# Gated cross-attention and a mixture of experts on one core: one transfer for means and factors, an earlier second batch, a rearranged passage

## The reference, cut to what matters

```python
# per batch: keys and values come from both the context and the rows
xn = layernorm(ctx, gamma_media, beta_media)          # (256, 256)
ln = layernorm(layernorm(x), gamma_lat, beta_lat)     # (256, 256)
q = ln @ Wq + bq;  k, v = split(concat([xn, ln]) @ Wkv + bkv)   # 8 heads of 128
attn = softmax(q @ k.T * 128 ** -0.5)                 # (256, 512) per head
x = x + tanh(g_xattn) * (attn @ v @ Wo + bo)
# mixture of experts, top 2 of 8, F = 1024
xh = layernorm(x)
w, idx = softmax(top_k(xh @ Wg + bg, 2))
y = sum over the two experts e of w_e * (silu(xh @ W1[e] + b1[e]) @ W2[e] + b2[e])
x = x + tanh(g_ffn) * y
```

## Time and profile before

| | |
|---|---|
| median of 3 runs | 1546.45 us (1545.08 to 1552.04) |
| the profiled execution | 1541.18 us, its span 1539.5 us |
| busy | PE 1491.3 us (97%), DVE 1140.1 (74%), ACT 954.1 (62%), POOL 568.9 (37%) |
| mean granted clock of TensorE | 0.994 |
| a 1 MB load of expert weights, issue to landing | 18.7 us (median of 45) |

### The profile page before, as it was taken

The page is one execution under the profiler, slowest core; times in us unless marked ns, Lnnn a source line. Parts: engine busy times, 40 slices in busy tenths (PEclk is TensorE's granted clock), DMA queues, the critical chain, the costliest instruction groups (busy, mean ns, idle before and its releaser), DMA issues. The chain is left out here.

```text
span 1539.5 us, 29848 instructions
## 1 busy us (share of the span) xinstructions
PE 1491.3 (97%) x10326; PEld 1371.1 (89%) x10326; DVE 1140.1 (74%) x2749; ACT 954.1 (62%) x2057; POOL 568.9 (37%) x654
## 2 busy tenths in 40 slices
PE   8699999999999999999999999999889999999996
PEld 6588898888888888888888989888889999999996
DVE  7567877778777787777778778787686666666685
ACT  6455556556555655655555565655787777777775
POOL 4213334233243333334233342332455454444442
PEclk9999999999999999999999999999999999999999
DMA  5101101011010111101011010012854455545463
GB/s 163 46 14 49 42 22 36 22 49 42 22 35 22 37 36 33 42 21 36 22 49 42 22 36 22 8 57 63 222 122 132 128 146 142 128 128 152 133 175 81
DMA packets 84465, 106.92 MB, mean 69 GB/s; under 512 B 25658, under 2 KB 69495, under 8 KB 84191
## 3 DMA queue, kind: packets, MB, share of 16 engines
q1 hardware_dynamic: 68350, 85.98, 18.1%
q0 software_dynamic: 15824, 18.98, 6.9%
q10 hardware_dynamic: 144, 0.05, 0.0%
HBM read 86.64 MB, written 18.35 MB: 68 GB/s over the span
## 5 line engine op out<-in xcount | busy, mean ns | idle before, releaser
L921 POOL TENSOR_SCALAR probs<-probs,rsum 128x512 f32<-128x512 f32 x256 | 175.1, 695 | 609.9 <-DVE rsum L1598 603.1
L1131 ACT ACTIVATE pt_hi<-turn 128x512 fp32r<-128x512 f32 x256 | 139.5, 597 | 235.1 <-PE turn L1278 233.6
L946 POOL DMA_INDIRECT out_rows<-yo,token x71 | 119.7, 1686 | 206.0 <-DMA out_rows<-yo,token 136.4
L1715 DVE TENSOR_TENSOR ht_lo<-hs,ht_hi 128x512 fp32r<-128x512 f32 x142 | 98.2, 692 | 119.6 <-ACT ht_hi L1098 117.9
L1030 ACT ACTIVATE probs<-score,nbias 128x512 f32<-128x512 f32 x256 | 173.6, 688 | 7.1 <-DVE nbias L1594 7.1
L1592 DVE TENSOR_REDUCE smax<-score 128x1 f32<-128x512 f32 x256 | 168.1, 683 | 7.0 <-PE score L188 6.8
L1089 ACT ACTIVATE hs<-ph,vecs 128x256 f32<-128x256 f32 (+1 forms) x284 | 114.8, 460 | 93.9 <-PE ph L188 86.2
L1835 DVE TENSOR_TENSOR pt_lo<-turn,pt_hi 128x512 fp32r<-128x512 f32 x256 | 164.3, 683 | 9.4 <-ACT pt_hi L1131 8.8
L186 PE MATMUL py<-w_hi,ht_lo 128*128 (+1 forms) x568 | 162.7, 286 | 4.2 <-DVE ht_lo L1715 2.6
L188 PE MATMUL py<-w_hi,ht_hi 128*128 (+1 forms) x568 | 160.6, 283 | 0.0
L187 PE MATMUL py<-w_lo,ht_hi 128*128 (+1 forms) x568 | 160.5, 283 | 0.0
(11 more groups left out here) (243 smaller groups left out, 4685.4 us busy)
## 6 DMA issues: line engine op xcount, KB each, us to landing
w_raw<-in_L_ffn_W SPq DMA_DIRECT2D x45, 1024.0 KB, 18.7
spread<-mean_and_factor SPq DMA_DIRECT2D x15, 512.0 KB, 4.1
xhat_rows<-rows SPq DMA_DIRECT2D x16, 264.0 KB, 2.2
x_raw<-in_x SPq DMA_DIRECT2D x16, 256.0 KB, 3.0
c_raw<-in_ctx SPq DMA_DIRECT2D x16, 256.0 KB, 3.3
out_rows<-x SPq DMA_DIRECT2D x16, 256.0 KB
z_turned<-in_x_turned SPq DMA_DIRECT2D x15, 256.0 KB, 3.8
z_turned<-in_ctx_turned SPq DMA_DIRECT2D x15, 256.0 KB, 4.2
```

What stands on the lines that cost most here:

```text
L921: last = pool.tensor_scalar(probs[n % 2][:, t, :], probs[n % 2][:, t, :], rsum[:, n % 2, t:t + 1], 1.0, ALU.mult, ALU.mult)
L946: pool.indirect_dma_start(out=A["out"], out_offset=bass.IndirectOffsetOnAxis(ap=token[:, u:u + 1].bitcast(U32), axis=0), in_=yo_of(t)[:, s ...
L1131: act.activation(pt[0][:, 2 * t:2 * t + 2, :], turn[t][:, :].rearrange("p (j i) -> p j i", j=2), ACT.Copy).then_inc(s_pthi, 1)
L1715: dve.tensor_tensor(lo[:, :], hs[n % N_HS][:, :], hi[:, :].bitcast(F32), ALU.subtract).then_inc(s_hlo, 1)
```

## The change

1. **One transfer.** `spread` becomes (128 partitions, 2, 4) a batch: `norms` goes out as it lies, in one DMA, and is read back broadcast. VectorE reads it with a stride of 8 elements. The halves of `zin` change places to match.
2. **Second batch sooner.** `load(2)` goes ahead of `spread_norms(1)`. For batch 1: centre and normalise in steps 2 and 3, scale in step 3, `split_kv(1)` in step 4.
3. **Queries' weights in three pieces.** `q1` covers 2 heads, a new `q2` 4 heads. High parts: o0 and q2 in step 1, o1 in step 2. Low parts: o0 in step 1, q2 in step 2, o1 in step 4.
4. **Passage.** In step 127 TensorE turns tile 0 ahead of the probabilities, ScalarE does `hi_x(0)` and two W2 pieces ahead of its output unit, VectorE `lo_x(0)` and `take_weights(0)` ahead of its own; `find_places(14)` and `take_weights(1)` move to step 128. `norm_rows(15)` splits: VectorE makes variance plus epsilon, GpSimd only the power, VectorE the two normalised rows. GpSimd issues `gather(2)` ahead of `list_tokens(14)`, `gather(3)` and `gather(4)` ahead of `list_tokens(15)`. Counts are read at n = 6 instead of 7, `find_rows` becomes `count_rows` (n = 7) and `find_late_rows` (n = 8), `weigh` goes to n = 9. Tile 5's split stands ahead of the W1 pieces in its step.
5. **W2 over time.** Pieces of places 2 to 7 are split over n = 15 to 63, the loads of places 4 to 7 are issued later, `out` waits only for the places that a tile can need.
6. **Additions.** A tile's two scatters have a semaphore each and wait for the tile before, not for one another.

```diff
+W2_SPLIT = {1: (1, 5), 2: (15, 19), 3: (20, 26), 4: (26, 32), 5: (32, 40), 6: (40, 48), 7: (48, 64)}
+W2_LOAD = {2: 5, 4: 6, 6: 7}
+W2_NEED = {1: 3, 3: 5, 5: 6, 7: 7, 11: 8}
...
-                for tiles, cols in ((slice(0, TT), slice(T, KEYS)), (slice(TT, JT), slice(0, T))):
-                        for r in range(2):
-                            sp.dma_start(dram["spread"][c, r, cols].rearrange("(j p) -> p j", p=P), norms[:, r, tiles])\
-                                .then_inc(s_norms_out, 16)
-                sp.wait_ge(s_norms_out, 64 * c)
+                sp.dma_start(dram["spread"][c], norms[:, :, :]).then_inc(s_norms_out, 16)
+                sp.wait_ge(s_norms_out, 16 * c)
...
             load_turned(1)
+            load(2)
             spread_norms(1)
...
-                    for at in range(2, E):
-                        load_w2(at)
+                    load_w2(2)
+                    load_w2(3)
...
+                if b == B - 1:
+                    load_w2(4)
...
+            sp.wait_ge(s_gathered(EARLY), 16 * gathered(EARLY))
             load_w1(EARLY + 1)
...
+                if t - EARLY in W2_LOAD:
+                    sp.wait_ge(s_w1lo, w1_before(t - N_RAW + 1) + PARTS // 2)
+                    load_w2(W2_LOAD[t - EARLY])
...
-                if u:
-                    pool.wait_ge(s_add, 16 * u)
+                if t:
+                    for half in range(SUB):
+                        pool.wait_ge(s_add[half], 16 * added(t, half))
...
-            for s in range(SUB):
-                gather(2, s)
-            norm_rows(B - 1)
+            pool.wait_ge(s_ve_last, 1)
+            pool.tensor_tensor(rs_c[:, 0:TT], ve["c"][:, 0:TT], minus_half[:, 0:TT], ALU.pow).then_inc(s_rsc, 1)
...
+                if i == STEPS - 1:
+                    hi_x(0)
+                    for q in W2_STEPS[i]:
+                        w2_hi(q)
...
             residual(B - 1)
+            dve.wait_ge(s_mvc, B)
+            dve.tensor_scalar(ve["c"][:, 0:TT], mv_c[:, 0:TT, 1], 1.0, EPS, ALU.mult, ALU.add).then_inc(s_ve_last, 1)
             lo_h(1)
+            dve.wait_ge(s_rsc, B)
+            dve.wait_ge(s_rowst[(B - 1) % 2], 16 * ((B - 1) // 2))
+            for t in range(TT):
+                last = dve.tensor_scalar(rows[(B - 1) % 2][:, t, 0:D], x2[(B - 1) % 2][:, t, :], mv_c[:, t, 0:1],
+                                         rs_c[:, t:t + 1], ALU.subtract, ALU.mult)
+            last.then_inc(s_xn, 1)
...
-                own.mark(dve.tensor_tensor(zin[:, k, :], zin[:, k, :], spread[:, 0, :], ALU.add))
+                by_rows = zin[:, k, :].rearrange("p (j i) -> p j i", j=JT)
+                own.mark(dve.tensor_tensor(by_rows, by_rows, spread[:, :, 0, :].rearrange("p i j -> p j i"), ALU.add))
```

More of the change, by code:

```diff
@@ L543, in layer @@
         W2_BEFORE = PARTS
+        w2_need = {step_of(EARLY + t): places * PARTS for t, places in W2_NEED.items()}
         def w2_by(n):
-            return W2_BEFORE + min(W2_PIECES - W2_BEFORE, n + max(0, n - 12))
+            return W2_BEFORE + sum(min(PARTS, max(0, n + 1 - first) * PARTS // (end - first))
+                                   for first, end in W2_SPLIT.values())
         def w2_piece(at, j):
@@ L627, in turned_of, with added @@
             return (routing, ph[(FIRST_N + 2) % N_PH])[(n - FIRST_N) % 2]
+        def added(t, half):
+            return min(t, WIDE) if half else t
         def by_step(function, t):
@@ L1002, in _ @@
                     ).then_inc(s_names, 16)
-                scatter(t - 1, 0)
-                if t == 1:
-                    list_tokens(B - 1)
-            pool.wait_ge(s_add, 16 * ROWS)
+                if t == 3:
+                    for s in range(SUB):
+                        gather(EARLY + 1, s)
+                if t > 1:
+                    for s in range(subs(t - 1)):
+                        scatter(t - 1, s)
+            for half in range(SUB):
+                pool.wait_ge(s_add[half], 16 * added(N_TILES, half))
         @program("scalar")
@@ L1175, in _ @@
                     e = expert_of(act, t)
+                if n in X_SPLIT and t + 1 == EARLY:
+                    hi_x(t + 1)
                 for part in w1_parts(n + LEAD):
                     w1_hi(*part)
-                if n in X_SPLIT:
+                if n in X_SPLIT and t + 1 != EARLY:
                     hi_x(t + 1)
@@ L1656, in find_rows, with find_late_rows, do @@
                 do(dve.tensor_reduce(wide_rows[:, :], length[:, 0:E], AX_X, ALU.add))
+            def find_late_rows():
+                def do(instruction):
+                    own.mark(instruction)
+                    own.wait()
+                own.wait()
                 do(dve.tensor_scalar(wide_rows[:, :], wide_rows[:, :], -1.0, float(LATE_WIDE), ALU.mult, ALU.add))
@@ L1840, in _ @@
                     lo_h(0)
+                    find_places(B - 2)
                 for u in steps[i]:
@@ L1857, in _ @@
                     reciprocal_sum(i)
-                if i in (3, 4):
-                    normalise_turned(1, i - 3)
+                if i == STEPS - 1:
+                    lo_x(0)
+                    take_weights(0)
+                if i in (2, 3):
+                    normalise_turned(1, i - 2)
                 for u in steps[i]:
@@ L1896, in _ @@
                 t, j = TILE_OF[n]
+                if n in X_SPLIT and t + 1 == EARLY:
+                    lo_x(t + 1)
                 for part in w1_parts(n + LEAD):
@@ L1912, in _ @@
                     choose(B - 1)
+                if n == 6:
+                    read_unit("r", B - 1)
+                    find_places(B - 1)
+                if n == 7:
+                    count_rows()
                 if n == 8:
-                    find_rows()
+                    find_late_rows()
+                if n == 9:
                     weigh(B - 1)
```

119 lines of the change are left out of this document (67 added, 52 removed).

## The result

| | before | after |
|---|---|---|
| median | 1547.96 us (4 runs, 1545.08 to 1552.04) | 1522.59 us (4 runs, 1521.97 to 1524.05) |
| profiled execution, its span | 1541.18 us, 1539.5 us | 1522.59 us, 1520.9 us |

The ratio is 0.9836, 95% interval 0.981 to 0.9861: faster by 25.4 us of median, where 25.5 was forecast (1521). That agreement is better than its parts. The two profiled executions lie only 18.6 us apart; the rest is that the kernel before runs 4 to 7 us longer outside its profile and the changed one does not. In a later group of runs the same two kernels had 1544.71 (9 runs) and 1517.23 us (5 runs), 27.5 apart. In a third group one execution of the kernel before took 3424 us, and is left out of that group's ratios. What follows takes the traces apart first, and then comes back to this.

A forecast was written before the change was run, and what follows sets the result against it. TensorE was taken to bound the kernel, busy 1491.3 of 1539.5 us, so gains come from its idle time or clock. Start 15.5 plus passage 10.0 gave 25.5 off 1546.45: 1521 us, range 1515 to 1525, 1513 to 1531 with two rivals.

The forecast's parts named there:

- `kt_lo` 5.0: Steps 1 to 3 of the start: TensorE's 6.7 us of waits for `kt_lo` become 1.6, a gain of 5.0.
- The wait of 1.18: Start, step 1: TensorE's 1.18 us wait for `kt_lo` goes to about 0.1, as q1's low part shrinks.
- `kvt_lo` 7.3: Batch 1's `v` unit: the whole 7.32 us wait for `kvt_lo` goes, its rows being ready near 60 us.
- Clock 3.7: Start: without TensorE's idle stretches of 4.1 and 7.3 us, the 1.7 and 2.0 us lost to low clock return.
- floor (1.2) and ceiling (9.4): Write of `spread`: 1.2 us as an eighth of the old 9.4; 9.4 if only the count of DMAs mattered.
- the slack argument: Steady batches: VectorE idles 0.36 and 0.43 us, so the first 0.79 us of extra per step are free.
- slower by the stride: Rival, chance 0.03: strided VectorE operations cost over 0.79 us extra; from 1.25 extra the 25.5 us gain is eaten.
- Forecast 10.0: Passage, 1040 to 1160 us: 10.9 us of waits and low clock go, less 0.9 of new waits; bounds 4 and 11.
- The rival of VectorE's wait for the power: Passage, chance 0.12: slow list DMAs make `lo_x(1)` 4 to 5 us late, clock falls; gain 19.5, 1527 us.
- Zero for both: W2 pieces moved to n = 15 to 63 hide there, and GpSimd has slack for scatters: no gain or loss.
- later the only wait is 0.30 us once a batch: TensorE in attention after the start, kernel before: a single wait of 0.30 us per batch, 14 times.
- 5.3 below the median: Profiled execution of the kernel before against its runs' median; no place in the trace, so left standing in the forecast.

The follow-up runs named there:

- kernel with filler: Changed kernel plus one unused 0.68 us VectorE operation ahead of each addition and multiplication from batch 2 on, 56 in all; 1519.69 us.
- passage-only kernel: Kernel before with only the passage, W2 over time and additions changes; 1533.21 us, ratio 0.99.
- kernel with GpSimd's rows: Changed kernel with the last batch's normalised rows back on GpSimd, nothing else moved; 1522.7 us.
- with four writes: Changed kernel with means and factors again leaving in four DMAs of 4-byte pieces and VectorE reading at unit stride; 1522.62 us.
- start-only: Kernel before with only the one transfer, sooner second batch and queries' weights in three pieces; 1532.85 us, ratio 0.9904.

## Why the prediction held, and where it did not

**Start.** Of its terms, `kt_lo` 5.0 measured 6.68 less 2.08, 4.6 us; but at another place than I had it. The wait of 1.18 did not go (1.15): VectorE did gain 1.07 us from the shorter low part of q1, and TensorE came 1.0 sooner too, since a wait of 1.02 at 28.5 us (labelled "issue", the `v` unit behind GpSimd's split of v1) went in the same step. GpSimd's 3.60 us for that split became 2.56 beside the shorter VectorE operation. `kvt_lo` 7.3: 6.97, less a new 0.16 behind it; the cover of 1.4 us that I counted was not there, since GpSimd's split took 3.24 us instead of 2.34, and TensorE waits 0.35. Clock 3.7: all of it. The 0.5 for the stride and a late `spread`: nothing, it was in when VectorE came. Together 4.6 + 1.0 + 6.8 + 3.7 = 16.1, forecast as 15.5. Part of this nearness is luck: the wait of step 0 stayed, where I had 1.1 us of it go, and the 1.0 at 28.5 us, which I hadn't counted, made up for it.

**The write.** I took 2.5 to 3.5 us between floor (1.2) and ceiling (9.4). It took 1.1, below the floor. The count of pieces fits both: 1024 pieces 9.4 us (8.1 a batch on average), 128 pieces 1.1, 8 to 9 ns each. The number of DMAs and the size of a piece changed with it, and no run parts them.

**The stride.** Between once and twice the price, as taken: 1.7 times. The kernel with filler shows that the slack argument stood, and had more room than I gave it. The Trainium skill ("SBUF — State Buffer", section "Door 1: The DMA port swizzle") wants consecutive accesses within one 16-byte line for full bandwidth; here a read 32 bytes apart took 1.16 us, 0.48 more than the 0.68 at unit stride, so the direction agrees, and the page has no factor to compare. The rival "slower by the stride" would have needed 1.25 us of extra.

**Passage.** Forecast 10.0 with 0.5 + 0.4 us of waits left; the passage-only kernel gave 9.9 of span, with 0.50 and 0.75 left, at the two places named. The rival of VectorE's wait for the power did not come at its size: `rs_c` kept VectorE 0.98 us, and TensorE then waited 0.7 for `xt_lo`, a wait that is gone in the kernel with GpSimd's rows; 0.4 was forecast.

**What failed.** First, the step "Zero for both" under parts 5 and 6. I priced the W2 pieces where they went, wide tiles with room, and not where they came from. Undoing part 5 alone costs 4.0 to 7.8 us of idle time in the passage, and the span is 5 to 10 us longer. The total did not suffer only because the waits which the pieces caused were already counted, all of them, under part 4. A reader who had taken part 4 alone for 10.0 us would have been wrong: with the pieces left where they were, 11.0 of the 11.4 us idle stayed. The new order gave next to nothing in the profiles while the pieces stood in it, and 10 us with them gone: that is the main thing that the sum had wrong.

Second, the step "later the only wait is 0.30 us once a batch", carried over to the changed kernel. All nine profiles with the new start and these loads in place have a wait of 1.95 to 3.84 us near 173 us (179 with four writes), behind a hole in ScalarE's work, which persists without the loads. What makes the hole stays open: a fetch of instructions was part of my theory, but the kernel with filler has the hole without a packet there. Why the old order passes that place without harm stays open too.

Third, the "5.3 below the median" that I left standing. It was not a constant. The kernel before runs above its profile (3.7 us in the second pair), the changed one does not (-0.4); the start-only and passage-only kernels stand between them, with spreads of 9 and 5 us, the changed one with 2. The clock goes with it: in the first group of experiments the timed runs of before have a mean clock of 0.991 at the median, against 0.994 in the first profile; 0.3% of 1540 us is 4.6 us, an estimate, of the 5.8 between them. Outside the profile, then, the change gives 27.5 us where the profiled pair gives 23.4. Long waits followed by a low clock are what the change removes, and such waits may be what varies, but no run shows one varying.

So 25.5 against 25.4 is made of terms that were right (16.1 and 9.7 us), less 2.0 at 173 us, less 5.0 for the gaps near 1101 us (2.6) with a late `xt_lo` (0.9) and the low clock behind them (1.5), less 1.4 for a clock of 0.86 and 0.79 at 5 to 15 us, which the profile of before does not have: 17.4, against 18.6 between the two profiles. Then come 6.8 us that only the timed runs of before pay. The unforeseen losses and this gain cancel by chance. That the "issue" gaps near 1101 us have a cause in the kernel's code is not excluded: they came in four profiles of two groups and in none of six others that run the same code there, and nothing that I changed goes with them.

One slip in the prediction's chances: its parts add up to 0.91 for faster and 0.03 for slower, where its summary has 0.90 and 0.04.

## What to carry to other kernels

When work leaves a crowded stretch, price it there first: 15 VectorE operations of 0.68 us that moved out of 80 us were what let the reordering of those that stayed pay at all. A strided read may be free where the engine idles, and idle stretches behind one another add up; but read the next steps' too. Transfers of tiny pieces cost, in both cases here, some 8 to 9 ns a piece, and everything that SyncE's program issues behind its wait for them pays as well: one layout that lets the write go out as it lies took 8.3 us out of it, and made a second reordering needless.

## What the runs showed of the hardware

- 4-byte pieces in four DMAs: 1024 in 9.4 us the first time, 8.1 on average over 15 batches; 128 pieces of 32 bytes in one DMA in 1.1 us; 8 to 9 ns a piece in both.
- A VectorE addition or multiplication of 128x512 in fp32 with one operand read 32 bytes apart: 1.11 to 1.23 us in all 60 operations (median 1.16 and 1.17), instead of 0.68.
- A 1 MB load of weights landed in 18.7 us (median of 45) in the first profile of the kernel before, in 5.1 in its second and in 5.3 in the changed kernel's: the figure belongs to the execution, not to the change, and a margin taken from one profile may be wrong by three times.
- ScalarE can stand for some 2 us with nothing to wait for that the profile shows (2.87 us at 168 us, where 0.72 is usual, with no load about); a packet of the instruction queue lies beside the hole in some profiles and is missing in one. TensorE then waits 1.2 to 1.6 us, and 1.95 to 3.84 with four 256 KB loads there.
- The same kernel has 1517.23 us in one group of runs and 1522.59 in another, each group within some 2 us: compare only inside a group.
